# Down tiles and output projection with high and low weights side by side in one bank

## What is computed

```
x = x + 0.5 * ffn(layernorm(x))     # ffn: gelu(x @ w1 + b1) @ w2 + b2, 256 -> 1024 -> 256
x = x + attn(layernorm(x))          # 16 heads of 64, causal, linear distance bias, softmax
                                    # attn ends in: out @ w_out + b_out, 1024 -> 256
x = x + 0.5 * ffn(layernorm(x))     # the same ffn weights again
```

## Time and profile before

| | |
|---|---|
| runs, us | 2213.71, 2218.69, 2223.47 (median 2218.69) |
| profiled execution, us | 2218.28 (span of its trace 2216.5) |
| granted TensorE clock in it, share of full | 0.991 |
| busy share: PE, PEld, DVE, ACT, POOL | 97%, 79%, 69%, 56%, 48% |

### The profile page before, as it was taken

One profiled execution on the slowest core, in us unless ns is written; L12 is line 12 of the kernel. 1 busy time (PEld: TensorE's weight loads), 2 busy tenths in 40 slices (PEclk: granted clock), 3 DMA queues, 4 the chain that ended last, 5 costly groups with the idle time before them and its releaser, 6 DMA issues.

```text
span 2216.5 us, 41791 instructions
## 1 busy us (share of the span) xinstructions
PE 2150.7 (97%) x14720; PEld 1743.0 (79%) x14720; DVE 1519.5 (69%) x4010; ACT 1234.5 (56%) x3092; POOL 1057.3 (48%) x1770
## 2 busy tenths in 40 slices
PE   6899999999999999999999999999999999999977
PEld 6578787877878778787887878778787887878857
DVE  6776867667676676776768676676766767667654
ACT  4655736456464664736557464564646547365552
POOL 1553716437273453725537174462635537264360
PEclk9999999999999999999999999999999999999998
DMA  3331505225051340514325052240513315043250
GB/s 128 105 96 53 134 25 139 72 69 141 3 159 52 94 117 25 157 30 118 93 60 133 18 140 71 85 126 9 155 48 108 103 35 152 25 130 81 58 143 10
DMA packets 109937, 193.91 MB, mean 87 GB/s; under 512 B 34464, under 2 KB 53152, under 8 KB 109728
## 3 DMA queue, kind: packets, MB, share of 16 engines
q1 hardware_dynamic: 89248, 138.77, 22.3%
q0 software_dynamic: 20480, 52.47, 9.6%
HBM read 14.95 MB, written 8.39 MB: 11 GB/s over the span
## 4 chain that ended last, share of the span: by engine, by line
PE 80%; ACT 8%; DVE 5%; POOL 4%; issue 2%; SPq 1%; DMA 0%; DVEq 0%; ACTq 0%; POOLq 0%
PE ps L272 79%; POOL P L880 3%; ACT P L562 3%; PE ps L326 2%; DVE P L730 2%; ACT gt L544 1%; DVE gl L652 1%; ACT L562 1%; SPq L222 1%; ACT qk L526 1%; DVE P L722 1%; ACT gh L548 0%; DVE x L681 0%; DVE wql L799 0%; POOL PT L222 0%
## 5 line engine op out<-in xcount | busy, mean ns | idle before, releaser
L880 POOL TENSOR_SCALAR P<-P,rs 128x512 f32<-128x512 f32 (+3 forms) x1024 | 541.7, 547 | 450.5 <-DVE rs L713 445.4
L562 ACT ACTIVATE P<-P,mx 128x512 f32<-128x512 f32 (+3 forms) x1024 | 562.5, 552 | 161.6 <-DVE mx L722 161.4
L222 POOL DMA_DIRECT2D PT<-P x640 | 322.8, 509 | 255.3 <-DVE P L730 237.2
L730 DVE STREAM_TRANSPOSE P<-P 128x1792 f32<-128x1792 f32 (+1 forms) x256 | 374.0, 1485 | 12.3 <-POOL P L880 11.8
L272 PE MATMUL ps<-PT,v 128*64 128x256 f32 (+1 forms) x3072 | 308.9, 351 | 18.3 <-DMA PT<-P 16.2
L272 PE MATMUL ps<-qk 64*128 64x512 f32 (+3 forms) x2048 | 313.2, 445 | 6.7 <-ACT qk L526 6.7
L272 PE MATMUL ps<-w2h,gh 128*128 128x256 f32 x1024 | 296.8, 290 | 9.0 <-DVE x L681 4.6
L526 ACT ACTIVATE qk<-ps 128x512 f32<-128x512 f32 x256 | 153.3, 599 | 271.1 <-PE ps L272 271.1
L272 PEld LDWEIGHTS ps<-PT,v 128*64 128x64 f32 x3072 | 205.8, 138 | 115.8 <-issue 25.8
L272 PE MATMUL ps<-w2l,gh 128*128 128x256 f32 x1024 | 289.5, 283 | 0.0
L272 PE MATMUL ps<-w2h,gl 128*128 128x256 f32 x1024 | 289.3, 283 | 0.0
(11 more groups left out here) (75 smaller groups left out, 4415.6 us busy)
## 6 DMA issues: line engine op xcount, KB each, us to landing
PT<-P SPq DMA_DIRECT2D x1408, 80.0 KB, 2.6
PT<-P POOLq DMA_DIRECT2D x640, 80.0 KB, 2.7
x<-in_L_attn_x SPq DMA_DIRECT2D x16, 512.0 KB, 4.2
out_y<-x SPq DMA_DIRECT2D x16, 512.0 KB, 3.2
raw<-in_L_ffn_w SPq DMA_DIRECT2D x2, 512.0 KB, 5.8
raw<-in_L_ffn_w SPq DMA_DIRECT2D x1, 1024.0 KB, 8.6
rawq<-in_L_attn_w_qkv SPq DMA_DIRECT2D x1, 1024.0 KB, 6.5
rawk<-in_L_attn_w_qkv SPq DMA_DIRECT2D x1, 1024.0 KB, 8.6
```

The costliest lines, as they stand in the source:

```text
L222: e.dma_start(PT[c % 2][32 * m:32 * m + 32, g, :], P[c % 3][32 * g:32 * g + 32, m, :]).then_inc(landed[c % 3].sem, 16)
L562: e.activation(p, p, ACT.Exp, bias=mx[:, r, i:i + 1], scale=-1.0, accum_out=sm[:, r, i:i + 1]).then_inc(s_ex.sem, 1)
L730: e.transpose(p, p).then_inc(s_tr.sem, 1)
L880: e.tensor_scalar(p, p, rs[:, 2 * (c % 2) + h, i:i + 1], 1.0, ALU.mult, ALU.mult).then_inc(s_nz.sem, 1)
```

## The change

High and low weights of `w2` lie side by side in one tensor (`w2`), and so do those of `w_out` (`wo`). For each m or c, one matmul of 512 columns streams both halves through the high part of the activations: high by high goes to the first half of the bank, high by low to the second. A second matmul, of 256 columns, adds low by high to the first half. In the last of the eight, the narrow one comes first. DVE then adds the second half of the bank to `x`, waits for that, and adds the first half. The signal that frees the bank comes with the second of these adds.

```diff
-    w2h, w2l = place("w2h", [128, NM, D], F32R), place("w2l", [128, NM, D], F32R)
+    w2 = place("w2", [128, 2, NM, D], F32R)
...
-    woh, wol = place("woh", [128, NC, D], F32R), place("wol", [128, NC, D], F32R)
+    wo = place("wo", [128, 2, NC, D], F32R)
+    w2h, w2l, woh, wol = (w[:, i, :, :] for w in (w2, wo) for i in range(2))
...
+            def wide(out, ah, al, b, first, last):
+
+                halves = out.rearrange("p (i n) -> p i n", i=2)
+                if last:
+                    mm(out[:, 0:D], al, b[:, 0, :], False, False)
+                    return mm(halves, ah, b, False, True)
+                mm(halves, ah, b, first, False)
+                return mm(out[:, 0:D], al, b[:, 0, :], False, False)
...
             def dn(f, b, t):
                 ts = slice(t * 128, t * 128 + 128)
-                dst = bank_for(("down", f, b, t))[:, 0:D]
+                dst = bank_for(("down", f, b, t))
                 for m in range(NM):
                     if t == 0:
                         e.wait_ge(s_gs.sem, s_gs.at((f, b, m)))
-                    g, l, wh, wl = gh[f][m][:, ts], gl[f][m][:, ts], w2h[:, m, :], w2l[:, m, :]
-                    mm(dst, g, wh, m == 0, False)
-                    mm(dst, g, wl, False, False)
-                    last = mm(dst, l, wh, False, m == NM - 1)
+                    last = wide(dst, gh[f][m][:, ts], gl[f][m][:, ts], w2[:, :, m, :], m == 0, m == NM - 1)
                 last.then_inc(s_dn.sem, 1)
...
-                dst = bank_for(("out", b, t))[:, 0:D]
+                dst = bank_for(("out", b, t))
                 e.wait_ge(s_ol.sem, s_ol.at((b, t)))
                 i = t % 3
-                last = three(dst, [(oh[i][:, c, :], ol[i][:, c, :], woh[:, c, :], wol[:, c, :])
-                                   for c in range(NC)])
+                for c in range(NC):
+                    last = wide(dst, oh[i][:, c, :], ol[i][:, c, :], wo[:, :, c, :], c == 0, c == NC - 1)
                 last.then_inc(s_ot.sem, 1)
...
             def add(events, key, produced, use, L, b, t):
                 e.wait_ge(produced.sem, produced.at(use[1:]))
                 e.wait_ge(s_pb.sem, s_pb.at((L, b)))
+                e.tensor_tensor(xb[b % 2][:, t, :], bank_of(use)[:, D:2 * D], xb[b % 2][:, t, :], ALU.add).then_inc(s_ra.sem, 1)
+                e.wait_ge(s_ra.sem, s_ra.at(use))
                 e.tensor_tensor(xb[b % 2][:, t, :], bank_of(use)[:, 0:D], xb[b % 2][:, t, :], ALU.add).then_inc(events.sem, 1)
                 e.wait_ge(events.sem, events.at(key))
```

More of the change, by code:

```diff
@@ L171, in build @@
     s_r2 = Signal("r2_done", outs)
+    added = [("down", 1, 0, t) for t in range(NT)]
+    for b in B:
+        if b > 0:
+            added += [("down", 2, b - 1, t) for t in range(NT)]
+        if b + 1 < NB:
+            added += [("down", 1, b + 1, t) for t in range(NT)]
+        added += [("out", b, t) for t in range(NT)]
+    added += [("down", 2, NB - 1, t) for t in range(NT)]
+    s_ra = Signal("low_part_added", added)
     s_bs = Signal("bs_done", counted)
```

## The result

The kernel with the change takes 2226.57 us (median of 6 runs, 2224.97 to 2230.12) against 2216.99 us of the kernel before in the same comparison (6 runs, 2213.71 to 2223.47): a ratio of 1.0035, 95% interval [1.0018, 1.0052] (the two medians alone would make 1.0043). So it is slower: the medians lie 9.6 us apart and the ratio makes 7.8, less than the half per cent that counted as no change, but clear of its interval. Its profiled execution, the fastest of the six, took 2224.97 us, 6.7 more than that of before; the other five have no trace. Three executions (one of e13, one of e15, one of the kernel before beside e11) ran at a granted clock of 0.65 to 0.75, took 2650 to 3013 us, and are left out of every figure here.

What follows compares the result with a forecast made beforehand. The prediction took PE as the bound in most stretches and an ACT and DVE chain in a few; turns of -2.4 us and +2.0 for both ends gave -0.4, so 2217 us, range 2208 to 2227.

Steps and rivals of the forecast that it cites:

- The pair: On PE, one 512-column and one 256-column matmul replace three of 256: 346.5 ns, saving 13.5 ns, 0.108 us a tile.
- the rival: On PE, the jump between halves costs: a wide matmul charged as two, 360 ns a pair, 2228 us; chance 0.10.
- The rival of the small fixed part: On PE, only 2.5 ns a pair saved, as the skill page's gap formula gives: 2226 us; chance 0.05.
- Beginning of a block: Down 2: second add delays the bank for tile 2 by 0.46 us, faster tiles return 0.22: +0.24 us a block.
- Down 1: Down 1: tiles 1 and 2 gain 0.216 us, tiles 0 and 3 nothing: -0.22 us a block.
- Output projection: Output projection: four faster tiles, with new waits taking part of the gain: -0.18 us a block.
- The wait for `ol` 1: Output projection, tile 1: the doubled add1 delays `ol` 1, so PE loses 0.12 us.
- The new wait at k0: After the output projection: PE waits for DVE's two `ln_lo`, k0 starting at about 305.9 instead of 305.77.
- Prologue: Before the first normalisation: four second adds of 0.46 us on DVE, with PE idle: +1.8 us.
- The turn: One block period: 0.24 - 0.22 - 0.18 us, 15 times, making -2.4 us.
- new waits of DVE's making: Sign that the forecast is wrong: such waits appearing in the attention pairs; no size given.
- another cover breaks: Rival at down 2 tile 3 and layernorm 3: second adds come through whole, 0.5 us a block, 2225; chance 0.08.

Runs made afterwards that it cites:

- e13: The kernel with the change, unedited, run a third time: 2224.25 us, ratio 1.0020 to the kernel before.
- e15: The kernel with the change plus a small DVE memset before the first cast of each block's down 1, except block 0 by its condition b > 0: 2224.39 us, 1.0015.
- e11: The kernel with the change, unedited, run a second time: 2217.42 us, ratio 1.0006 to the kernel before.
- e3: The kernel with the change, DVE's adds of down 2 tile 1 moved before the long transpose of probabilities: 2209.74 us, ratio 0.9968.
- e7: The kernel with the change, POOL's bias of the next block moved one pair of heads earlier: 2208.70 us, ratio 0.9968.
- e8: The kernel before, POOL's bias of the next block moved one pair of heads earlier: 2204.83 us, ratio 0.9949.
- e4: The kernel before, DVE's add of down 2 tile 1 moved before the long transpose of probabilities: 2210.89 us, ratio 0.9973.
- e6: The kernel before with DVE's add done twice, so that `x` gets each tile twice, without wide matmuls: 2226.66 us, ratio 1.0056.
- e2: The kernel before, POOL's bias of the next block moved behind the last normalisations of probabilities: 2224.04 us, ratio 1.0030.
- e14: The kernel with the change, bias one pair of heads earlier (e7 again), run beside e13: 2209.08 us, ratio 0.9945.
- e5: The kernel with the change without the second add, so high by low is left out of `x`: 2207.72 us, ratio 0.9963.
- e17: The change in down 1 and output projection only, plus down 2 tile 1's add before the transpose and bias one pair earlier: 2197.47 us, ratio 0.9908.
- e18: The kernel before with down 2 tile 1's add before the transpose and the bias one pair earlier: 2199.07 us, ratio 0.9917.
- e1: The kernel with the change, POOL's bias of the next block moved behind the last normalisations of probabilities: 2228.61 us, ratio 1.0051.

## Why the prediction was right and wrong

**The number.** 2217.0 was forecast, 2226.57 measured. The range, to 2227, holds it; the forecast of no difference was within the half per cent but missed a real loss of 8 to 10 us. Two executions without a lost cast gave 2217.42 and 2218.65. Most terms of the forecast can be found again in them, below; that the range held the median of 2226.57 is luck, since no term of it stood for a lost cast.

**The pair: mis-sized, and small.** 346.5 ns was taken from the sum of the two steady paces; it measured 350.8 in the mean. A tile gains 0.06 to 0.08 us, not 0.108. The width change is paid more often than I took it: a strict alternation has no long runs, and the 234 ns of the earlier trace rows was the better price for a wide one behind a narrow one. The saving itself was rounded up, too: with 119.5 ns instead of 120 it is 12.5 ns a pair. The jump in the moving operand costs nothing that the traces show: the wide one's step, 234 ns, is that of a 512 without a jump in the earlier trace rows, and the rival wanted 360 a pair. The rival of the small fixed part is down as well. The formula that the prediction set beside it from the Trainium skill, page TensorE: Matmul & The Clock Gate, section Back-to-back issue gap, is given there for an isolated matmul, and not for a stream with a weight load for each, as this one is.

**Beginning of a block: right.** +0.34 us against +0.24 (medians of 14 turns, from the first `up` to the scores behind tile 3: 31.22 and 31.56), with the wait at tile 2 longer by 0.58 us and its chain by 0.47 (0.46 forecast). Tile 3 had the slack that was counted; e3 shows it used up.

**Down 1: right where no cast is lost.** -0.18 us against -0.22 (15.07 and 14.89), by the smaller gain of a tile. Tile 3 gained nothing, as forecast.

**Output projection: right sum, one wait wrong.** -0.17 us (12.45 and 12.28 from the first output tile to k0), where -0.18 was forecast. The wait for `ol` 1 came. The new wait at k0 did not. The two `ln_lo` ended at 305.30 (DVE's line below), 11.90 us behind the first output tile at 293.40, where I had them 12.16 behind it (305.80 - 293.64), and k0 started when PE got there, 12.24 behind it. PE was later than I had it by its slower pairs, so the right sum is in part luck:

```profile
304.04 1.26 DVE L668 TENSOR_TENSOR xtl<-ps,xth 128x512 fp32r<-128x512 f32 x2
...
305.64 0.39 PE L282 MATMUL ps<-xth,wqh 128*128 128x512 f32 x1
```

**Prologue: right.** The k0 projection of block 0 starts 1.5 us later (48.05 against 46.53); 1.8 was forecast. In this trace it was made up for before the first output tile, at which after is 0.18 ahead; in e7 against e8, 1.4 of it stays. The pattern of all 15 turns didn't fit the last one, which takes 131.45 us against 130.09.

**The turn.** -0.16 us forecast, -0.04 measured (134.00 against 134.04). Without a lost cast that leaves about no change: e11 is +1.4 us by its median, within its interval.

**The step that failed** is the price of DVE's other instructions. I counted where DVE's adds are awaited and took every other instruction of DVE to cost what it cost in the one trace before. In down 1 that put the first cast of the gelu splits at 0.77 us and its wait for POOL's run at nothing more, without a reason. The trace shows it at 4.26 and 4.27 us in two blocks, which cost 3.4 and 2.0 us in their down 1 stretches (and 2.1 us in block 11 of e15). Taken off, they bring 2224.97 to 2219.6; most of what is left above 2217.42 and 2218.65 lies in the last turn (131.45 us against 129.83 and 130.29). The sign "new waits of DVE's making" was named, but only as a sign of a wrong price, not as a mechanism with a place; "another cover breaks" had the right size (2225) and the wrong places.

It is not shown that the change brings these lost casts about. The obvious way, that the second adds and the faster tiles move DVE against POOL, is ruled out at this place: in the ten traces that keep the bias where it was, the cast starts 2.46 to 2.48 us into POOL's run (2.55 in e15, by its memset), with the change or without. Lost casts are in 2 of the 7 traces with wide matmuls (after, e15) and in none of the 3 without (before, e4, e6), which is too few to part the two kernels.

The Trainium skill, page SBUF — State Buffer, section Who interferes with whom, says of the port pair that DVE and GpSimd share that the one that issues first has it for the whole instruction and the other fully blocks. The traces agree as to blocking: the cast of e2 began 0.39 us behind the start of POOL's bias and ended at 955.17, 0.29 us behind the bias's end at 954.88. They differ in its length in the lost casts: the one at 403.95 did not end with the POOL instruction then running but waited through the end of POOL's run, five instructions in a row, so the price of a collision here was POOL's run and not its current instruction.

**What stays open.** What decides the race is not known, nor whether the change makes it be lost more often. That lost casts make an execution slower is shown by four traces of the change and its near copy (two lost: 2224.97 and 2222.80 us; none: 2217.42 and 2218.65); the narrow spread of e14 fits that. The other five executions of the first comparison (2225.10 to 2230.12) and the slowest of e13 have no trace, so for them it is inferred. A rival stands untested: the kernel before has one trace without edits, and its slower executions (to 2223.47, and to 2226.52 beside e13) may have lost casts as well. Why the clock fell behind one lost cast and not behind the other, with the same stalls, is open too.

## What to carry to other kernels

A saving of one engine is only worth its share up to the next wait that another sets: e5 shows 13 us of pace on PE shrink to 8 with nothing added at all. Before an edit adds work to DVE, look in the timeline for the places where DVE and POOL work on SBUF side by side and ask which runs of POOL are gapless and how long they are, because there the same instruction at the same place took 0.8 us in one execution and 4 in another. One trace shows one outcome of such a race: take a second one before you call its price fixed. Long POOL instructions belong where DVE has nothing urgent: one line of order was worth 11 us in the kernel before (e8), where the best use of the change, e17 against e18, was worth 1.6.

## What the runs showed of the hardware

- A cast of 128x512 on DVE, 0.76 to 0.80 us beside POOL's run and 0.38 to 0.43 undisturbed, took 4.26 us when it waited through a gapless run of five POOL instructions; in the same program this came not at all (e11, e13) or twice (after), with the same distance of the starts.
- A subtraction with two SBUF inputs on DVE takes 0.69 us alone and 1.80 when it meets POOL's 2.4 us addition (e11); two of them took 4.06 (e1), and a cast 2.31 (e2).
- Alternating fp32r matmuls of 512 and 256 columns step at 350.8 ns a pair in the mean at 2.4 GHz (234 and 117), where the steady paces add up to 346.5; a moving operand in two runs of 256 elements costs nothing in addition.
- After PE had been busy for 1.88 of 3.00 us the granted clock was 0.53 for the next 3.60 us; after 1.89 of 3.00 us with the same stalls, 138 us later, it stayed at 1.00.
